# Overflow rows of two binned groups in one scatter, plain masks in one operation, index rows in fewer loads: a graph-network kernel on one core

## The reference

```python
# x (6250, 64); src, dst (206250,), sorted by dst; edge_attr (206250, 64)
h = relu(layernorm(x))
e = concat([h[dst], edge_attr], axis=1)
e = relu(e @ W1.T + b1)                       # 128 wide
e = relu(e @ W2.T + b2)                       # 128 wide
summed = segment_sum(e, src, 6250)            # src is in random order
cnt    = segment_sum(1, src, 6250)
agg = summed / max(cnt, 1)
z = relu(concat([h, agg, u0]) @ Wa.T + ba)
out = x + z @ Wb.T + bb
```

## Time and profile before

| | us |
|---|---|
| median of 3 runs | 2166.95 (2166.85 to 2167.39) |
| the profiled execution, device time | 2171.31 |
| its span | 2169.6 |
| busy PE / DVE / ACT / POOL | 1828.7 / 1555.7 / 743.1 / 1713.9 |

### The profile page before, as it was taken

One profiled execution on the slowest core, in us unless ns is written; L12 is line 12 of the kernel. 1 busy time (PEld: TensorE's weight loads), 2 busy tenths in 40 slices (PEclk: granted clock), 3 DMA queues, 4 the chain that ended last, 5 costly groups with the idle time before them and its releaser, 6 DMA issues.

```text
span 2169.6 us, 44519 instructions
## 1 busy us (share of the span) xinstructions
PE 1828.7 (84%) x12535; PEld 1545.1 (71%) x12535; DVE 1555.7 (72%) x5312; ACT 743.1 (34%) x1779; POOL 1713.9 (79%) x1100
## 2 busy tenths in 40 slices
PE   3798888898999899998989999899899997677717
PEld 2576766787787787777777787788787886566615
DVE  8876666777777787777777787777777886455418
ACT  3243433333334343333333443333333332111103
POOL 5288888888888888888888888888888888888850
PEclk8799999999999999999999999999999999788859
DMA  7798888999999999998999999999999999687756
GB/s 282 225 181 165 160 158 158 186 203 201 200 197 195 195 205 207 199 208 176 207 195 196 202 196 204 205 193 198 202 195 208 202 218 198 92 140 129 112 109 187
DMA packets 395312, 406.30 MB, mean 187 GB/s; under 512 B 51933, under 2 KB 294269, under 8 KB 394557
## 3 DMA queue, kind: packets, MB, share of 16 engines
q1 hardware_dynamic: 241164, 332.21, 53.9%
q0 software_dynamic: 152640, 70.08, 34.3%
q10 hardware_dynamic: 1264, 1.11, 0.2%
HBM read 226.75 MB, written 176.44 MB: 186 GB/s over the span
## 4 chain that ended last, share of the span: by engine, by line
POOL 63%; issue 25%; DVE 5%; PE 4%; DMA 3%; SPq 1%; ACT 0%; POOLq 0%; ACTq 0%; DVEq 0%
POOL sums L719 49%; POOL sums L707 13%; DMA sums<-regA,idx 2%; PE bank L1142 1%; PE bank L1166 1%; PE bank L1120 1%; DVE regC L1020 1%; DVE regC L890 1%; DVE regC L1031 1%; DVE regC L896 0%; DMA regC<-in_src_cols 0%; PE bank L1156 0%; DVE regC L1021 0%; DVE regC L1022 0%; DVE regC L901 0%
## 5 line engine op out<-in xcount | busy, mean ns | idle before, releaser
L719 POOL DMA_INDIRECT sums<-regA,idx x876 | 1385.7, 1582 | 321.0 <-issue 263.5
L999 DVE TENSOR_TENSOR h<-bank,b2n 128x512 f32<-128x512 f32 x403 | 278.8, 692 | 419.9 <-PE bank L1166 283.3
L1120 PEld LDWEIGHTS bank<-h,regC 128*128 128x128 f32 x2944 | 385.7, 201 | 239.8 <-issue 223.1
L1120 PE MATMUL bank<-h,regC 128*128 128x130 f32 x2944 | 420.9, 288 | 120.6 <-ACT h L811 78.6
L1166 PE MATMUL bank<-w,h 128*128 128x128 f32 x3224 | 454.5, 287 | 0.0
L1142 PE MATMUL bank<-regA,L 128*128 128x512 f32 x806 | 422.0, 606 | 2.6 <-DVE regA L940 2.0
L1166 PEld LDWEIGHTS bank<-w,h 128*128 128x128 f32 x3224 | 420.7, 204 | 1.1 <-ACT h L796 0.6
L790 ACT ACTIVATE regC<-bank 128x260 f32<-128x260 f32 x736 | 285.3, 388 | 256.9 <-PE bank L1120 148.1
L1156 PEld LDWEIGHTS bank<-h,regC 128*128 128x128 f32 x1752 | 239.1, 200 | 188.0 <-issue 184.6
L804 ACT ACTIVATE regA<-bank 128x516 f32<-128x516 f32 x219 | 131.7, 601 | 690.6 <-DMA sums<-regA,idx 589.6
L796 ACT ACTIVATE h<-bank 128x512 f32<-128x512 f32 x403 | 240.1, 596 | 306.3 <-PE bank L1142 187.4
(11 more groups left out here) (130 smaller groups left out, 1223.9 us busy)
## 6 DMA issues: line engine op xcount, KB each, us to landing
regC<-slots SPq DMA_DIRECT2D x245, 260.0 KB
regA<-in_ea SPq DMA_DIRECT2D x202, 256.0 KB
slots<-regC SPq DMA_DIRECT2D x184, 260.0 KB
slots<-regC SPq DMA_DIRECT2D x184, 203.1 KB
src<-rows_src SPq DMA_DIRECT2D x219, 128.0 KB
dstR<-rows_dst SPq DMA_DIRECT2D x403, 64.0 KB
sums<-regA,idx POOLq DMA_INDIRECT x876
sums<-zeros SPq DMA_DIRECT2D x20, 645.0 KB, 8.4
```

What stands on the lines that cost most here:

```text
L719: nc.gpsimd.indirect_dma_start(out=sums[k], out_offset=bass.IndirectOffsetOnAxis(ap=idx[:, n % RING, t:t + 1], axis=0), in_=scat[:, n % 4, ...
L999: VE.tensor_tensor(h2[:, g % 2, :, 0:H], psL2(g % 2).rearrange("p (t f) -> p t f", t=TPG), b2n[:, :].unsqueeze(1).broadcast_to([P, TPG, H] ...
L1120: last = T.matmul(psSlot(t)[:, k, :], place, h2[:, g % 2, t, :], start=True, stop=True)
```

## The change

Five edits go together.

1. Overflow: the four tiles of a binned group share 60 overflow places (before: 32 for each tile). They are the first 60 of the 256 places. A second small reduction on DVE, `earlier`, and a second small matmul let the count run on from tile to tile. DVE adds the four tiles' overflow parts to one (`vpre`, 60x130), and SP copies that from SBUF to half of `V`. The mask, the matmuls, ACT's copy and the scatter are made once for two binned groups (`closes`).
2. The masks of a plain group are one equality of 128x512, without the triangle and the counts. A column of powers of two that fall from partition to partition (`weight`) stands beside `h2`; in its sum an edge sees whether an earlier one has the same `src`. `extra` and `idx` are made from `scat`, so after ACT's evacuation.
3. The `dst` rows are stored as bytes and loaded for four groups at once, the `src` rows for two plain groups at once; both have two buffers.
4. `slots` no longer holds overflow: 68 and 128 rows are written per group instead of 128 and 100.
5. The test that chooses the general branch (not taken before) is made on four tiles together.

```diff
-OVER = 32
-SLOTS = NBIN * CAP + OVER
+OVER = 60
+PLACES = NBIN * CAP
+HEAD = P - OVER
+def closes(g):
+    return is_sorted(g) and BINNED_NO[g] % 2 == 1
@@ SP
-                    wait(sp, oh_ready, s - 3)
-                    sp.dma_start(dB[D:P, s % 4, :], rows_dst[s].partition_broadcast(P - D)).then_inc(dB_in[s % 4], 16)
+                    if s % GPP == 0:
+                        i = s // GPP
+                        wait(sp, oh_ready, GPP * (i - 1))
+                        sp.dma_start(dB[D:P, i % 2, :, :]..., rows_dst[i].partition_broadcast(P - D)).then_inc(dB_in[i % 2], 16)
-                    for k in range(2):
-                        rows = min(P, SLOTS - k * P)
-                        sp.dma_start(slots[n, k * P:k * P + rows, :], slot_sb[0:rows, n % 2, k, :, :]...)
+                    sp.dma_start(slots[n, 0:HEAD, :], slot_sb[OVER:P, n % 2, 0, :, :]...)
+                    sp.dma_start(slots[n, HEAD:PLACES, :], slot_sb[:, n % 2, 1, :, :]...)
-                    sp.dma_start(V[:, n % 2, :], slots[n, SLOTS - OVER:SLOTS, :]...)
+                    sp.wait_ge(vpre_ready, n + 1)
+                    sp.dma_start(V[half * OVER:(half + 1) * OVER, j % 2, :], vpre[:, half, :]).then_inc(v_in[n % 4], 16)
@@ POOL
-                if is_sorted(s - VLAG):
+                if closes(s - VLAG):
@@ DVE
+                    VE.tensor_reduce(earlier[:, n % 2, :], flags_before(n % 2), axis=AX.X, op=ALU.add).then_inc(earlier_ready, 1)
-                    for t in range(TPG):
-                        mask = VE.scalar_tensor_tensor(out=S[:, n % 4, t, :], in0=sB[...], scalar=srcF[...],
-                                                       in1=tri[:, :], op0=ALU.is_equal, op1=ALU.mult, accum_out=cnt[:, n % RING, t:t + 1])
+                    VE.tensor_tensor(S[:, n % 4, :, :], sB_of(g)..., srcF[...]..., ALU.is_equal).then_inc(mask_ready, 1)
-                if is_plain(s):
+                if is_plain(s - 3):
+                    dve.wait_ge(scat_ready, n + 1)
+                    VE.scalar_tensor_tensor(out=extra[:, n % 2, :], in0=scat[:, n % 4, :, C], scalar=weight25[:, :], in1=toscrap[...], op0=ALU.is_gt, op1=ALU.mult)
+                if is_sorted(s - VPRE):
+                    dve.wait_ge(slot_ready, TPG * (n + 1))
+                    VE.tensor_reduce(vpre[:, n % 2, :], slot_sb[0:OVER, n % 2, 0, :, :].rearrange("p t c -> p c t"), axis=AX.X, op=ALU.add)
@@ PE
-                    T.matmul(psOver, prefix[:, :], over[:, n % 2, :], start=True, stop=True).then_inc(over_done, 1)
+                    T.matmul(psOver, prefix[:, :], over[:, n % 2, TPG - 1:2 * TPG - 1], start=True, stop=False)
+                    pe.wait_ge(earlier_ready, n + 1)
+                    T.matmul(psOver, onesb[:, :], earlier[:, n % 2, :], start=False, stop=True).then_inc(over_done, 1)
```

More of the change, by code:

```diff
@@ L81, with src_row, row_pairs @@
 NH = len(BINNED)
+NV = NH // 2
 BLOCKS = [BINNED[k:k + BLOCK] for k in range(0, NH, BLOCK)]
+def src_row(g):
+    return g // GPP * GPP + 2 * (g % 2) + g // 2 % 2
+def row_pairs():
+    pairs = {}
+    for g in PLAIN:
+        pairs.setdefault(src_row(g) // 2, []).append(g)
+    return list(pairs.values())
+ROW_PAIRS = row_pairs()
+ROW_PAIR_AT = {pair[0]: m for m, pair in enumerate(ROW_PAIRS)}
+ROW_PAIR_OF = {g: m for m, pair in enumerate(ROW_PAIRS) for g in pair}
+def closes(g):
+    return is_sorted(g) and BINNED_NO[g] % 2 == 1
 def scatter_table():
@@ L116 @@
 STEPS = max(max(UNITS_AT) + 2, NG + VSUM + 1)
-CONSTS = 16
-DERIVED = 8
+CONSTS = 17
+DERIVED = 10
+TOP = 190 << 23
 XBB_STEP = 200
@@ L242, in build @@
         rank = sb("rank", [P, 2, TPG], f32)
-        over = sb("over", [P, 2, TPG], bf16)
+        over = sb("over", [P, 2, 2 * TPG - 1], bf16)
+        earlier = sb("earlier", [P, 2, TPG], bf16)
+        vpre = sb("vpre", [OVER, 2, W], f32)
         V = sb("V", [P, 2, W], f32)
@@ L915, in _, with sB_of, flags_before @@
             dve.wait_ge(tiles_psum, 1)
-            link(VE.memset(perm[:, :, :, SLOTS:PW], 0.0))
+            link(VE.memset(over[:, :, :], 0.0))
+            link(VE.memset(V[:, :, :], 0.0))
+            def sB_of(g):
+                return sB[:, ROW_PAIR_OF[g] % 2, src_row(g) % 2, :]
+            def flags_before(k):
+                row = over[:, k, 0:TPG].copy()
+                return bass.AP(row.tensor, row.offset, [list(row.ap[0]), [1, TPG], [1, TPG - 1]])
             def add_unit(k, q):
@@ L979, in _ @@
+                if is_plain(s - 3):
+                    n = PLAIN_NO[s - 3]
+                    dve.wait_ge(scat_ready, n + 1)
+                    VE.scalar_tensor_tensor(out=extra[:, n % 2, :], in0=scat[:, n % 4, :, C], scalar=weight25[:, :], in1=toscrap[:, TPG * (s - 3):TPG * (s - 2)],
                                             op0=ALU.is_gt, op1=ALU.mult).then_inc(extra_ready, 1)
-                if is_plain(s - 1):
-                    n = PLAIN_NO[s - 1]
                     dve.wait_ge(extra_ready, n + 1)
-                    wait(dve, scat_ready, n - 3)
-                    VE.tensor_tensor(idx[:, n % RING, :], extra[:, n % 2, :], srcF[:, TPG * (s - 1):TPG * s], ALU.add).then_inc(idx_ready, 1)
@@ L985, in _ @@
-                if is_sorted(s - VMASK):
-                    n = BINNED_NO[s - VMASK]
-                    dve.wait_ge(vmask_ready, n + 1)
-                    VE.scalar_tensor_tensor(out=vextra[:, n % 2:n % 2 + 1], in0=vcnt[:, n % 2:n % 2 + 1], scalar=1.5, in1=scrapc[:, :],
-                                            op0=ALU.is_gt, op1=ALU.mult).then_inc(vextra_ready, 1)
-                    dve.wait_ge(vextra_ready, n + 1)
-                    wait(dve, vscat_ready, n - 1)
-                    VE.tensor_tensor(vidx[:, n % 6:n % 6 + 1], vextra[:, n % 2:n % 2 + 1], V[:, n % 2, C:W], ALU.max).then_inc(vidx_ready, 1)
+                    VE.tensor_tensor(idx[:, n % RING, :], extra[:, n % 2, :], srcF[:, TPG * (s - 3):TPG * (s - 2)], ALU.add).then_inc(idx_ready, 1)
@@ new lines, in _ @@
+                if closes(s - VMASK):
+                    j = BINNED_NO[s - VMASK] // 2
+                    dve.wait_ge(vmask_ready, j + 1)
+                    VE.scalar_tensor_tensor(out=vextra[:, j % 2:j % 2 + 1], in0=vcnt[:, j % 2:j % 2 + 1], scalar=1.5, in1=scrapc[:, :],
+                                            op0=ALU.is_gt, op1=ALU.mult).then_inc(vextra_ready, 1)
+                    dve.wait_ge(vextra_ready, j + 1)
+                    wait(dve, vscat_ready, j - 1)
+                    VE.tensor_tensor(vidx[:, j % 6:j % 6 + 1], vextra[:, j % 2:j % 2 + 1], V[:, j % 2, C:W], ALU.max).then_inc(vidx_ready, 1)
@@ L1097, in free_row @@
             def free_row(s):
-                wait(pe, vmask_ready, sum(1 for g in BINNED if g <= s - VBC - 1))
+                wait(pe, vmask_ready, sum(1 for g in BINNED if closes(g) and g <= s - VBC - 1))
             def bin_tile(g, t, general):
```

200 lines of the change are left out of this document (113 added, 87 removed).

## The result

The changed kernel takes 2030.61 us (median of 4 runs, 2028.74 to 2031.52), the kernel before 2166.9 us beside it: a ratio of 0.937, 95% interval 0.9359 to 0.9381. It is 136 us faster. The forecast was 1994 us with a range of 1975 to 2050: the sign and the range held, but 37 us of the gain that the sum promised did not come, and the time lies next to the price of a rival (2037).

The account below looks back on a forecast made before the run. POOL's scatters were taken to bound the kernel: 2171.3 us profiled less 176.1 for 92 scatters is 1995.2, the runs' median 4.4 below gives 1990.8, plus 3 for lost margin makes 1994 us; range 1975 to 2050.

Parts of the forecast that it names:

- What bounds the kernel before, and what a scatter costs.: POOL's scatters bind the kernel before, at 1.892 us each; dropping 92 overflow scatters takes 176.1 us off POOL's list.
- The start: Before the first scatter: POOL waits for zeroing to 98.91 us anyway, so the change costs nothing, within 3 us.
- POOL stays the bound, by 1%.: Pairs of groups: PE and DVE's chain averages 8.44 us a pair over a block, against 8.51 of POOL.
- the first rival: PE and DVE's chain binds: pairs with a unit at 9.5 us, average 8.87, 43 us lost, 2037 us; chance 0.22.
- The case that POOL goes on binding: POOL's list of scatters still sets the pace after the change: 1975 to 2006 us, chance 0.66.
- The prediction's low end: Scatters on POOL: half of some 35 us of disturbance gone would give 1994 - 18, about 1975 us.
- the 3 that were allowed: 3 us added to the sum for places where the 1% margin is lost for a while.
- POOL's lag of 27 us covers that.: Fifth block: PE and DVE fall 11 us short of POOL's pace; POOL's lag covers it, so nothing is lost.
- Loads at nothing, covered by SP running ahead.: New waits of row loads on SP cost nothing, since loads are issued some five groups (20 us) ahead.
- The slower rivals: Few DMA engines bind (0.05, 2198 us); DVE's new wait adds up (0.02, 2266); general branch runs (0.01, 3,000 us more).
- DVE's new wait at `extra`: DVE waits for ACT's evacuation; half of ACT's 3.1 us in series gives 10.0 a pair, 2266 us; chance 0.02.
- few DMA engines bind: SP's store of 68 rows goes to four DMA engines only, 9.63 us a pair, +31 us, 2198; chance 0.05.

Follow-up runs that it names:

- masks_undone: The changed kernel with plain masks again made in four operations with triangle and counts, `extra` and `idx` from the counts in their old places: 2032.8 us, 0.9372.

## Why the prediction was right, and where it missed

*What bounds the kernel before, and what a scatter costs.* Right. The 92 scatters were worth 176 us on POOL's list: at 1.892 us for each that remains, 965 would have taken 1826 us; they took 1857, from 97.3 to 1954.2. The last sums are evacuated and the last scatter issued as far apart as in the earlier trace rows, by the changed kernel's timelines:

```profile
1926.96 0.60 ACT L845 ACTIVATE regA<-bank 128x520 f32<-128x520 f32 x1 [7.32 <-DMA sums<-regA,idx]
```

```profile
1952.68 1.55 POOL L758 DMA_INDIRECT sums<-regA,idx  x1 [0.30 <-issue]
```

That is 1954.2 - 1926.96 = 27.3 us of lag, as the prediction said the tail would build up again. The start, too: the last table was zeroed by 97.32 us instead of 98.91, within the 3 us given.

*"POOL stays the bound, by 1%."* This is the step that failed. Where units stand in 25 of 32 pairs (400 to 1500 us) the chain through PE and DVE needs 8.65 us a pair, not 8.44, and it binds; POOL needs 4.5 x (914.30 / 572 + 0.305) = 8.57, not 8.51. What came about is the mechanism of the first rival, which had a chance of 0.22, at a pace of 8.65 instead of its 8.87, and only in the blocks with units: the first block went by POOL as forecast. The case that POOL goes on binding had 0.66 and ended at 2006; the measured time is in the range only because the range was drawn on to 2050 for this rival. That the rival's own time, 2037, lies so close is in part luck: it put 46 + 24 us into the two stretches with units and took 27 of lag off, where the runs show 18 + 11 and no lag. A margin of 1% was smaller than the error of either price. The sizes behind it:

- `vpre` was priced at 0.70 us between bounds of 0.36 and 0.97 and takes 1.06, above both. The run without three quarters of it is 15 us faster and comes within 0.04 us a pair of POOL's need.
- That price came from a slope between a reduction and an operation that isn't one, and neither has a stride.
- DVE's sum was taken from its share of the whole span, 6.8 us a pair, and put at 7.2 for the changed kernel. From 400 to 1600 us it was 919.62 / 127 = 7.24 before and is 1087.69 / 138.2 = 7.87 now: 0.63 more where 0.4 were counted.
- The rest of the chain's missing 0.21 us isn't split further. `earlier` was priced right: 0.17 us, and 0.30 between the small matmul and the unit instead of 0.06.
- Scatters were left at their length, and they became 1.601 us for 1.586. Where the chain binds this costs nothing now; it leaves 0.08 us a pair at most to gain. The prediction's low end had counted on shorter ones.
- One equality takes 0.69 us for the 0.64 given. Its gain stood in DVE's sum, and is worth nothing in time.
- The median lies 1.9 us above the profiled execution, where the prediction took 4.4 off: 6 us of the 37.

Together: 18 us in the blocks with units, 11 in the fifth, 1 or 2 in the tail (the 31 us between 1857 and 1826), 6 between profiled execution and median, 2 behind the last scatter; less the 3 that were allowed. That is 36 of the 37.

*"POOL's lag of 27 us covers that."* This failed too, and follows from the same step. The fifth block was priced at 9.0 and 8.95 us a pair and takes 9.00, so the price was right, and the prediction named the 11 us that it would cost without the lag. But where the chain binds no lag is left at its start: ACT stands 20 us for landings from 400 to 1600 us, where it stood 366 before.

*"Loads at nothing, covered by SP running ahead."* The number was right, the reason only half, and that was luck. The prediction listed what the edit removes and never priced the new copy in SP's list. Without the fewer loads the kernel would be at 2185 us, slower than before: a way to the other side that none of the rivals named.

*The slower rivals.* DVE's new wait at `extra` didn't add up: undoing it (`masks_undone`) changes nothing. That few DMA engines bind finds no support: the DMA share is 0.93 where units stand, at 192 GB/s, for 0.95 and 199 before. (The prediction's sum of bytes saved was off: 64 + 65 + 34.5 + 32.3 make 196 KB a pair, not 187, and its next sum does use 196.) No run split the store of 68 rows, so what it costs by itself stays open.

*What stays open:* whether `vpre` as contiguous additions would be cheaper (not tried), and why moving it between steps never helped.

## What to carry to other kernels

When a sum says that the bound stays by 1%, the second limit is the forecast as much as the first: price it with the same care, stretch by stretch, and don't price a strided operation from rows of contiguous ones. Price each new DMA in the list of the engine that issues it, not only in bytes: with two more loads a pair on SP, moving one copy of 0.9 us to another engine's list gave back 155 us. Lag that is to cover a later stretch has to be there when it begins: ask which stretch before it keeps it. And work that is shortened beside slack gives nothing; undo one part at a time to see which part pays.

## What was not expected of the hardware

- The reduction of 520 elements, with the reduced ones 130 apart, takes 1.057 us on DVE, that of 130 elements 0.274: 2.0 ns for each element more, against 1.04 between the two contiguous rows of the prediction (a reduction of 196 and an operation on 784).
- SP is held 0.92 us by the issue of one SBUF to SBUF copy over 60 partitions, and 0.33 by a copy of the same tile from DRAM.
- An indirect DMA on POOL takes longer when it meets a DVE multiplication by a constant with one SBUF input (1.617 us for 1.582 of the others) or an addition with two (1.621 for 1.586), not when it meets a memset (1.562 for 1.593) or the reduction `vpre` (1.558 for 1.618). The time grows by 0.6% in both cases with inputs.
